# Attention cores of a four-layer transformer kernel: scores of a tile in two PSUM banks with two buffers, block-diagonal keys written by ScalarE two tiles at a time

## What is computed

```python
q = (query @ Wq.T + bq).reshape(b, tq, 16, 8)
k = (key @ Wk.T + bk).reshape(b, tk, 16, 8)
v = (value @ Wv.T + bv).reshape(b, tk, 16, 8)
score = jnp.einsum('bqhd,bkhd->bhqk', q, k) / np.sqrt(8)
score = jnp.where(causal, score, -jnp.inf)
probs = jax.nn.softmax(score, axis=-1)
out = jnp.einsum('bhqk,bkhd->bqhd', probs, v).reshape(b, tq, 128)
x = x + out @ Wo.T + bo
```

## Time and profile before

| | |
|---|---|
| median of three runs | 4139.28 us |
| the profiled execution | 4151.76 us |
| its span in the trace | 4150.2 us, 70163 instructions |
| TensorE busy | 2838.8 us (68%) |
| VectorE busy | 2431.9 us (59%) |
| ScalarE busy | 987.5 us (24%) |
| GpSimd busy | 754.8 us (18%) |
| mean granted TensorE clock | 0.822 of full speed |

### The profile page before, as it was taken

How to read it: one execution, slowest core, us unless ns; L and a number is a source line. 1 busy time by engine, 2 the same in 40 slices (tenths; PEclk the granted TensorE clock), 3 DMA queues, 4 the chain that set the end, 5 groups by cost and what they waited for, 6 DMA issues and landing times. The chain is left out here.

```text
span 4150.2 us, 70163 instructions
## 1 busy us (share of the span) xinstructions
PE 2838.8 (68%) x24814; PEld 1993.3 (48%) x24860; DVE 2431.9 (59%) x5688; ACT 987.5 (24%) x1360; POOL 754.8 (18%) x1395
## 2 busy tenths in 40 slices
PE   6783336788599999999966777565074067688246
PEld 3552224566466666666545555454053056466126
DVE  4438994688445555555444789545000455789668
ACT  1223332344100000000022344333021011344140
POOL 0001220344100000000000244111603400344003
PEclk7766557899799999999987889887597577899568
DMA  2000003000222112212100000100121122000001
GB/s 65 15 10 9 0 0 69 18 0 0 82 82 82 60 64 81 81 51 71 41 25 18 3 0 0 47 0 0 59 74 53 34 61 53 2 0 0 6 0 41
DMA packets 119629, 140.93 MB, mean 34 GB/s; under 512 B 75747, under 2 KB 87779, under 8 KB 118502
## 3 DMA queue, kind: packets, MB, share of 16 engines
q1 hardware_dynamic: 111718, 118.07, 9.2%
q0 software_dynamic: 7808, 21.52, 1.7%
HBM read 122.26 MB, written 17.30 MB: 34 GB/s over the span
## 5 line engine op out<-in xcount | busy, mean ns | idle before, releaser
L1114 PE MATMUL banks<-l1f_xe,l1f_w 128*128 128x512 f32 x1024 | 486.6, 598 | 11.4 <-DVE l1f_xe L1313 11.4
L1313 DVE TENSOR_TENSOR l1f_xe<-l1f_hT,l1f_rwb 128x512 f32<-128x512 f32 x256 | 173.4, 693 | 301.0 <-PE banks L1116 277.8
L1116 PEld LDWEIGHTS banks<-l1f_w,l1f_xe 128*128 128x128 f32 x2048 | 269.6, 192 | 123.5 <-issue 123.5
L1116 PE MATMUL banks<-l1f_w,l1f_xe 128*128 128x128 f32 x2048 | 270.3, 275 | 0.0
L1319 DVE TENSOR_TENSOR l1f_ae<-l1f_aoT,l1f_rwb 128x512 f32<-128x512 f32 x256 | 172.8, 690 | 160.2 <-PE banks L1144 155.9
L1114 PEld LDWEIGHTS banks<-l1f_xe,l1f_w 128*128 128x128 f32 x1024 | 177.0, 192 | 142.0 <-issue 126.8
L1144 PE MATMUL banks<-l1f_ae,l1f_w 128*128 128x512 f32 x512 | 225.2, 598 | 1.4 <-DVE l1f_ae L1319 1.4
L214 POOL COPY x<-xn 128x512 f32 (+1 forms) x64 | 39.0, 610 | 1016.4 <-DVE xn L1343 973.0
L223 PE MATMUL banks<-consts,l3p_h 128*128 128x128 f32 x64 | 17.8, 433 | 212.4 <-DVE l3p_h L140 212.4
L2389 DVE TENSOR_TENSOR l2e_y<-banks,l2e_sets 128x512 f32<-128x512 f32 x16 | 11.1, 692 | 253.0 <-PE banks L2362 253.0
L1144 PEld LDWEIGHTS banks<-l1f_ae,l1f_w 128*128 128x128 f32 x512 | 97.1, 192 | 118.2 <-issue 116.0
(11 more groups left out here) (460 smaller groups left out, 6916.0 us busy)
## 6 DMA issues: line engine op xcount, KB each, us to landing
l1f_rwb<-l1f_shares SPq DMA_DIRECT2D x128, 512.0 KB, 4.6
l1p_ctx<-in_ctxT SPq DMA_DIRECT2D x32, 256.0 KB, 3.6
l3p_ctx<-in_ctxT SPq DMA_DIRECT2D x32, 256.0 KB
l2e_sets<-in_L_ffn_expert_sets POOLq DMA_DIRECT2D x8, 578.0 KB, 4.7
l0a_ctxT<-in_ctxT SPq DMA_DIRECT2D x16, 256.0 KB, 2.8
l2p_ctxT<-in_ctxT SPq DMA_DIRECT2D x16, 256.0 KB, 2.7
l2f_sent<-l2g_zero SPq DMA_DIRECT2D x4, 1024.0 KB, 8.4
l2e_rows<-l2f_sent SPq DMA_DIRECT2D x16, 256.0 KB, 2.8
```

The lines of the kernel that those rows point to most:

```text
L1114: pe.matmul(bank, w[:, n, e, :], xe[:, e % NB, :], start=(e == 0), stop=(e == E - 1))
L1116: last = pe.matmul(v_bank[:, D * j:D * j + D], xe[:, e % NB, P * j:P * j + P], w[:, 2, e, :], start=(e == 0 and j == 0), stop=(e == E - 1) ...
L1313: dve.tensor_tensor(xe[:, e % NB, :], hT[:, m, :], rwb[:, m, e, :], ALU.mult).then_inc(s.xe_ready, 1)
```

## The change

Scores go into two full banks per tile (heads 0 to 7 from channels 0 to 63, heads 8 to 15 from channels 64 to 127), tiles alternate between banks 0, 1 and banks 2, 3. `score` waits for `centred` of the tile two before. The eight score matmuls of 32 rows and 256 moving columns become four of 64 rows and 512 moving columns; the four mask matmuls of 256 columns become two of 512. The keys are no longer spread by GpSimd: ScalarE does it in a new part `spread_k` with lag 0, last in its list, four scaled copies of 128x256 elements in each tile, for heads 0 to 3 of a pair of tiles in the even tile and for heads 4 to 7 in the odd tile, after which `k_ready` counts two tiles. All lags on TensorE, ScalarE and VectorE grow by one.

```diff
@@ attention_core
-        kbd = sb("kbd", [P, 2, 2, 4, S])
+        kbd = sb("kbd", [P, 2, 8, 2 * P])
-        top = sb("top", [P, 16])
+        top = sb("top", [P, 2, 16])
...
-        scores = k.banks[:, 0:4, 0:4 * S].rearrange("p a (b n) -> p a b n", n=S)
+        def scores(par):
+            return k.banks[:, 2 * par:2 * par + 2, :].rearrange("p a (h n) -> p (a h) n", n=S)
...
                 wait(pool, s.score_psum, t - 1)
                 settle(pool, k)
-                pool.tensor_tensor(kbd[:, par],
-                                   r.kT[:, bass.ds(P * t, P)].rearrange("p (b n) -> p b n", b=2).unsqueeze(2).to_broadcast([P, 2, 4, S]),
-                                   k.headmask.unsqueeze(1).unsqueeze(3).to_broadcast([P, 2, 4, S]), ALU.mult)
                 pool.tensor_copy(qT[:, par], r.qT[:, bass.ds(P * t, P)]).then_inc(s.q_ready, 1)
...
             def score(t, j):
                 par = j % 2
                 pe.wait_ge(s.q_ready, t + 1)
-                wait(pe, s.centred, t)
+                pe.wait_ge(s.k_ready, t - j % 2 + 2)
+                wait(pe, s.centred, t - 1)
+                banks = ps[2 * par:2 * par + 2]
                 if mask:
                     rhs = mask.rhs(pe, t, par)
-                    for a in range(4):
-                        pe.matmul(scores[:, a], k.identb[:, :], rhs, start=True, stop=False, skip_group_check=True)
-                for a in range(4):
-                    lo = 32 * a
+                    for bank in banks:
+                        pe.matmul(bank, k.identb[:, :], rhs, start=True, stop=False, skip_group_check=True)
+                else:
+                    settle(pe, k)
+                for a in range(2):
+                    rows = slice(64 * a, 64 * a + 64)
                     for b in range(2):
-                        last = pe.matmul(scores[S * b:S * b + S, a].rearrange("p h n -> p (h n)"),
-                                         qT[lo:lo + 32, par, S * b:S * b + S],
-                                         kbd[lo:lo + 32, par, b].rearrange("p h n -> p (h n)"), start=not mask, stop=True,
+                        seq = slice(S * b, S * b + S)
+                        keys = slice(P * (j % 2) + S * b, P * (j % 2) + S * b + S)
+                        last = pe.matmul(banks[a][seq, :], qT[rows, par, seq], kbd[rows, j // 2, :, keys], start=not mask, stop=True,
                                          skip_group_check=True)
...
-            pipeline(pe, k.NT, [(1, score), (2, turn), (4, project), (3, weigh)], unroll=TG)
+            pipeline(pe, k.NT, [(2, score), (3, turn), (5, project), (4, weigh)], unroll=TG)
...
+            def spread_k(t, j):
+
+                part, at = j % 2, t - j % 2
+                wait(act, s.score_psum, at - 2)
+                settle(act, k)
+                for n in range(4 * part, 4 * part + 4):
+                    last = act.activation(kbd[:, j // 2, n, :], r.kT[:, bass.ds(P * at, 2 * P)], ACT.Copy, scale=k.headmask8[:, n:n + 1])
+                if part == 1:
+                    last.then_inc(s.k_ready, 2)
...
-            pipeline(act, k.NT, [(2, copy_pT), (1, exp)], unroll=TG)
+            pipeline(act, k.NT, [(3, copy_pT), (2, exp), (0, spread_k)], unroll=TG)
...
-                dve.tensor_reduce(top[:, :].rearrange("p (a b) -> p a b", a=4), scores, AX_X, ALU.max).then_inc(s.max_ready, 1)
+                dve.tensor_reduce(top[:, par], scores(par), AX_X, ALU.max).then_inc(s.max_ready, 1)
...
-            pipeline(dve, k.NT, [(1, centre), (3, normalise), (4, new_x)], unroll=TG)
+            pipeline(dve, k.NT, [(2, centre), (4, normalise), (5, new_x)], unroll=TG)
```

More of the change, by code:

```diff
@@ L669, in attention_core @@
         s = sems(nc, ctx, name, "biased xn_ready stats_chain stats_ready mv_copied weights cleared q_ready v_ready score_psum max_ready "
-                 "centred exp_ready pT_psum pT_ready o_psum rec_ready o_ready y_psum")
+                 "k_ready centred exp_ready pT_psum pT_ready o_psum rec_ready o_ready y_psum")
         wo = sb("wo", [P, D])
         orow = sb("orow", [P, D])
-        kbd = sb("kbd", [P, 2, 2, 4, S])
+        kbd = sb("kbd", [P, 2, 8, 2 * P])
         qT = sb("qT", [P, 2, P])
         vbd = sb("vbd", [P, 2, 2, H // 2, 32])
-        top = sb("top", [P, 16])
+        top = sb("top", [P, 2, 16])
         prob = sb("prob", [P, 2, 16, S])
@@ L819, in centre @@
                 dve.wait_ge(s.score_psum, t + 1)
-                dve.tensor_reduce(top[:, :].rearrange("p (a b) -> p a b", a=4), scores, AX_X, ALU.max).then_inc(s.max_ready, 1)
+                dve.tensor_reduce(top[:, par], scores(par), AX_X, ALU.max).then_inc(s.max_ready, 1)
                 dve.wait_ge(s.max_ready, t + 1)
                 wait(dve, s.pT_psum, t - 1)
-                dve.tensor_tensor(prob[:, par].rearrange("p (a b) n -> p a b n", a=4), scores,
-                                  top[:, :].rearrange("p (a b) -> p a b", a=4).unsqueeze(3).to_broadcast([P, 4, 4, S]),
+                dve.tensor_tensor(prob[:, par], scores(par), top[:, par].unsqueeze(2).to_broadcast([P, 16, S]),
                                   ALU.subtract).then_inc(s.centred, 1)
@@ L980, in phase_l1_attention @@
         l1_projections(nc, k, r)
-        mask = Mask(rhs=lambda pe, t, par: k.causalb[:, :])
+        mask = Mask(rhs=lambda pe, t, par: k.causalb[:, 0:S].unsqueeze(1).to_broadcast([P, 8, S]))
         attention_core(nc, k, "l1a", r, float(HD) ** -0.5, "L1_xattn_WoT", mask, "L1_xattn_bo")
@@ L1745, in rhs @@
             pe.wait_ge(ready, t + 1)
-            return mask_b[:, par].unsqueeze(1).to_broadcast([P, 4, S])
+            return mask_b[:, par].unsqueeze(1).to_broadcast([P, 8, S])
         attention_core(nc, k, "l3a", r, float(HD) ** -0.5, "L3_xattn_Wo", Mask(rhs=rhs, copy=copy))
@@ L2458, in constant_parts @@
         "causal2": np.where((n[None, :] % P // S == p[:, None] // S) & (n[None, :] % S <= p[:, None] % S), 0.0, NEG),
-        "headmask": (p[:, None] % 32) // HD == np.arange(4)[None, :],
         "causal": np.where(np.arange(4 * S)[None, :] % S > p[:, None] % S, NEG, 0.0),
         "headblock": p[:, None] // HD == n[None, :] // HD,
+        "headmask8": (p[:, None] % 64) // HD == np.arange(8)[None, :],
         "pairsum": n[None, :64] % 32 // HD == 2 * (n[None, :64] // 32) + p[:, None] // S,
@@ L2516, in build_program @@
         k.causal2 = constant("causal2")
-        k.headmask = constant("headmask")
         k.causal = constant("causal")
         k.headblock = constant("headblock")
+        k.headmask8 = constant("headmask8")
         k.pairsum = constant("pairsum")
```

## The result

The changed kernel takes **4561.92 us** (median of 4 runs, 4559.87 to 4568.75); the kernel before took 4141.4 on the same chip. The ratio is 1.101, 95% interval 1.0988 to 1.1038: slower by a tenth, where 4506 (4355 to 4690) had been forecast. The profiled execution took 4568.75 us, its span 4567.2, which is 417.0 more than the span before.

The account below looks back on a forecast made before the run. The loop was taken to be nearly VectorE's, losing mostly the maximum's wait for scores. Longer steps and core starts (+263 us) and clock falls (+104) on 4139 gave 4506 us, range 4355 to 4690.

Parts of the forecast that it names:

- key copy: On ScalarE, one scaled copy of 128x256 in spread_k: 0.49 us.
- four in a row: On ScalarE, a tile's four key copies one after another: 1.65 us with the semaphore, bounds 1.16 to 1.93.
- scores: On TensorE, a tile's four wide score matmuls side by side: 1.16 us at full clock, 2.10 at half.
- step into an even tile: Maximum to maximum, through subtraction, exp, key copies, mask and scores: 7.15 us in layers 1 and 3, 6.6 in layer 2.
- into an odd one: Step whose scores only follow weigh on TensorE: 4.0 us in layers 1 and 3; VectorE's 3.6 in layer 2.
- +263: Loss of the three cores at full clock in us: +254 from longer steps, +9 from the cores' starts.
- +104: Loss in us from TensorE's clock falling behind long waits: two falls per group, 2.2 us over 47.25 groups.
- +367: Whole forecast loss in us, +263 at full clock and +104 for the clock, added to 4139.
- Rival 1: Same order of ScalarE's list, but TensorE's clock stays full: 4402 us; chance 0.17.
- Rival 2: TensorE at half clock throughout the cores, steps of 8.5 and 7.2 us: 4715 us; chance 0.11.
- Rival 3: TensorE's 64-row matmuls don't run side by side, 0.94 us more per step that TensorE decides: 4636 us; chance 0.06.
- Rival 4: ScalarE is a pair of tiles ahead with the keys, so TensorE never waits for them: 4099 us; chance 0.04.

Follow-up runs that it names:

- e1: Changed kernel with spread_k first instead of last in ScalarE's list; 4115.86 us, ratio 0.9917 to the kernel before.
- e2: Changed kernel with the four key copies of every odd tile written once more into a spare tile; 4728.24 us.
- e3: Changed kernel with the four key copies of every even tile written once more into a spare tile; 4592.3 us.
- e4: Changed kernel with 26 unread matmuls on TensorE before its wait for the keys of each even tile; 4399.14 us, ratio 1.0598 to the kernel before.
- e8: e1 with copy_mv last instead of first in GpSimd's list; 4133.03 us, ratio 0.9958 to the kernel before.
- e9: Changed kernel with keys written by GpSimd instead of ScalarE, and copy_mv last in GpSimd's list; 4127.64 us, ratio 0.9949 to the kernel before.
- e7: e1 with turn (the transposes) last in TensorE's list; 4111.27 us, ratio 0.9915 to the kernel before.
- e10: Kernel before the change with copy_mv last instead of first in GpSimd's list; 4150.56 us against 4151.18, ratio 0.9999.

## Why the prediction was right

**The mechanism.** The order of ScalarE's list decides, as forecast: the steps alternate, 114.5 us of TensorE's idle before the mask in layer 1 end with the key copies, and e1 removes all of the loss by that order alone. e2 and e3 show that only the copies behind exp count.

**The terms at full clock.** Forecast and measured: key copy 0.49 and 0.493; four in a row 1.65 and 1.69; scores 1.16 and 1.09 (2.10 and 1.99 at half clock); step into an even tile 7.15 and 6.99; into an odd one 4.0 and 3.88 (e4; 4.46 to 5.22 in the changed kernel, where the step before it ran at half clock); with `new_x` 5.7 and 5.9. For the copies, rows 7 to 9 left 1.16 to 1.93; the value near the middle was a choice between these bounds, and that it held is partly luck. The Trainium skill, page "ScalarE: Activation LUTs", section "What ACT_TABLE_LOAD costs", gives 186 ns and 0.833 per element, about 93 ns for each operand per partition, and an overlap of 93 between neighbours. By that, an estimate from the page's figures, one copy is 492 ns and four are 1.69 us; the trace agrees (0.493, 1.69). At full clock three cores of 381, 357 and 381 us (with the start) had been expected; e4 measured 369.5, 352.6 and 368.6. So +263 was 29 too much. Groups of 23.7 instead of 24.0 in layers 1 and 3 make 31.5 x 0.3 = 9 of it; the rest is the start and end of a core: 3 us had been added to 15.75 groups, and e4's cores are 3 to 4 us shorter than 15.75 of their groups.

**The step that was mis-sized is the clock.** It had been put at two falls of 1.1 us in each group, +104. The runs show 189 us in the cores between the changed kernel and e4 (163 between the medians, as e4 ran on another chip and is 19 us longer outside of the cores). The number of falls was nearly right: in layer 2 the clock is low behind both long waits of each group, in layer 1 behind three of four. Their price was not. In layer 2 a group takes 27.3 us for e4's 22.6, that is 2.35 for each fall; in layer 1 two groups take 54.6 for e4's 47.4, that is 2.4 for each of three falls. The 1.1 had been taken from the kernel before, as the mean loss of a group; there the clock is back before the transposes end (they take 1.60 to 1.67 us in the groups with a fall, 1.97 at half clock throughout). Here mask, scores and transposes at 1.2 GHz add 0.43 + 0.90 + 0.88 = 2.2 us, and all three stand in the chain of that step or of the next. The errors go against each other (29 too much at full clock, 85 too little for the clock), so it is partly luck that the sum, +367 forecast and +422 in the cores, looks better than its larger term.

**The rivals.** Rival 1, the clock stays full, is the kernel e4: 4402 had been worked out, 4399 came. That it is so near is luck: of the 260 us over 4139 the cores have 234, for 263 forecast, and the rest lies outside of them and in the chip. For the change itself it is wrong by its clock, 0.75 to 0.80. Rival 2, half clock throughout, lies 153 us too high: the clock comes back in every group. In layer 1 the mask of each odd tile but the first takes 0.60 us, and so does that of every fourth even tile, behind a wait of 3.04 (the timeline at 991.31). That is where the trace and the Trainium skill ("TensorE: Matmul & The Clock Gate", section "HAM oscillation") part a little: in the kernel that the page tells of, each burst behind its long wait for data begins slow; here behind waits of 3.04 us some do (963.10) and some don't (991.31), while behind all of 4.8 us and more they do. The page's remedy is to restructure the loop so that TensorE keeps its clock; here e1 does this by the order of one list (0.99 to 1.00), and e4 gets the same clock by filling the wait. Rival 3, 64-row matmuls one after the other, is out with 1.09 us for the four score matmuls. Rival 4, ScalarE a pair ahead, is nearly e1: 4099 and groups of 17.7 and 16.5 for it, 4116 and 17.8 and 17.0 measured. In the changed kernel it is out, since the keys were waited for in every pair.

**What stays open.** Why a wait of one length lets the clock fall in one group and not in the next was not settled; the runs show a clock of 0.99 to 1.00 where the waits are filled (e4) or under 1 us in the steady groups of layer 1 (e1), 0.96 to 0.99 in layer 1 with one of 1.81 in each group (e8, e9), and 0.75 to 0.80 with waits of 3 and 5 us (the changed kernel). The cause of e8's loss against e1 stays open with it. In e1 a maximum still waits 0.3 to 0.5 us for the scores in two steps of four, though VectorE is the fuller engine; e7 tried one order of TensorE's list and changed nothing, and no other was tried.

## What to carry to other kernels

Where each engine runs a fixed list of stages, a new stage is placed by what it waits for: what depends on nothing recent goes ahead of what waits for this step's work, else its consumers wait for that too, and a second buffer buys nothing. Price a moved stage by the chain it stands in, not by busy time: the same 162 us of copies cost 30 in one round and 166 in the other. When a long wait is opened on TensorE, add what its clock loses behind it at the length of the chain that then runs slow; and when a wait is taken away, look at the clock again (e8). Before a wait is taken away at all, read in the trace what ended it last: in the kernel before it was VectorE, not q (e10).

## What was not expected of the hardware

- 26 matmuls per pair of tiles that compute nothing of use made the kernel 163 us faster (4561.9 to 4399.1 us), by the clock: 0.75 to 0.80 became 1.00.
- A single wait of 1.81 us was followed by transposes at 1.89 us (e8), while behind one of 3.04 us the mask ran at full clock (0.60) in one group and at half (1.03) in another. The length of the last wait alone doesn't tell.
- Four score matmuls of 64 rows, 64 columns and 512 elements side by side take 1.09 us, half of the bound for two rounds of them (2.10).
- GpSimd's product of 128x1024 took 1.90 us for 1.04 at 128x512: one wide instruction takes 0.18 less than two of 1.04.
